# Third layer's adjacency counting in finer steps, and the sum rounds' one-hots by eight operations per batch

## The reference

```
# third: relational sum, 8 relations
xW  = einsum('ni,rio->nro', x, W)                       # W mixed from basis_w
agg = segment_sum(xW[src, etype], dst)
h   = relu(agg + x @ loop_w + bias) + relu(x @ res_w + res_b)     # then a batch norm
# fourth: two plain mean aggregations
mean = segment_sum(x[src], dst) / max(deg, 1)
y    = mean @ W_l.T + b + x @ W_r.T                     # relu after the first
```

## Time and profile before

| | |
|---|---|
| median of 3 runs | 6375.03 us (6363.15 to 6378.08) |
| the profiled execution | 6382.97 us, of which the span of instructions is 6381.1 us |
| PE, PEld, DVE, ACT, POOL busy | 4386.8, 3624.8, 2671.0, 1784.3, 4172.8 us |
| gathers of POOL | 4160, 3.9 ms of busy time |

### The profile page before, as it was taken

The page is one execution under the profiler, slowest core; times in us unless marked ns, Lnnn a source line. Parts: engine busy times, 40 slices in busy tenths (PEclk is TensorE's granted clock), DMA queues, the critical chain, the costliest instruction groups (busy, mean ns, idle before and its releaser), DMA issues. The chain is left out here.

```text
span 6381.1 us, 116473 instructions
## 1 busy us (share of the span) xinstructions
PE 4386.8 (69%) x25432; PEld 3624.8 (57%) x25433; DVE 2671.0 (42%) x9398; ACT 1784.3 (28%) x5020; POOL 4172.8 (65%) x4271
## 2 busy tenths in 40 slices
PE   4488888878877785666666765565555557776776
PEld 3377777767776774555555554444444445555554
DVE  6643333333333332666666553433344352223222
ACT  0022222222222223444444353333333330001001
POOL 3067777757777773777777656555555537776777
PEclk6599999999999996555666677777777779898988
DMA  3066666642222212333333322222222224444443
GB/s 78 3 171 158 154 158 157 156 113 53 53 53 53 53 52 47 87 84 83 83 85 83 81 60 75 72 68 63 72 73 73 71 95 139 139 132 131 132 139 101
DMA packets 383128, 595.38 MB, mean 93 GB/s; under 512 B 120483, under 2 KB 289988, under 8 KB 372420
## 3 DMA queue, kind: packets, MB, share of 16 engines
q0 software_dynamic: 133120, 276.30, 16.9%
q1 hardware_dynamic: 245156, 310.79, 16.5%
q10 hardware_dynamic: 4128, 1.75, 0.1%
HBM read 519.07 MB, written 69.42 MB: 92 GB/s over the span
## 5 line engine op out<-in xcount | busy, mean ns | idle before, releaser
L1404 PE MATMUL PS<-ROOM 128*128 128x128 f32 x8320 | 1058.4, 287 | 171.9 <-ACT ROOM L1010 103.5
L1404 PEld LDWEIGHTS PS<-ROOM 128*128 128x128 f32 x8320 | 999.2, 199 | 237.4 <-ACT ROOM L1010 124.1
L839 POOL DMA_INDIRECT GB<-table,IDX x832 | 801.1, 963 | 393.6 <-issue 245.9
L1010 ACT COPY ROOM<-PS 128x512 f32<-128x512 f32 x1040 | 609.9, 586 | 890.5 <-PE PS L1418 890.1
L839 POOL DMA_INDIRECT ROOM<-table,IDX x416 | 402.7, 968 | 376.4 <-ACT IDX L986 252.2
L839 POOL DMA_INDIRECT GB<-in_x,IDX x416 | 402.9, 969 | 370.8 <-ACT IDX L986 234.7
L2058 DVE TENSOR_TENSOR ROOM<-ROOM,PS 128x128 f32 x312 | 89.6, 287 | 1121.4 <-PE PS L1429 1107.2
L811 POOL DMA_INDIRECT GB<-table,IDX x416 | 417.0, 1002 | 170.9 <-issue 125.2
L1346 PE MATMUL PS<-PACK 128*128 128x300 bf16 x624 | 186.8, 396 | 479.3 <-ACT SPARE L981 253.7
L799 POOL DMA_INDIRECT GB<-table_gat,IDX x416 | 429.1, 1032 | 127.7 <-issue 124.7
L811 POOL DMA_INDIRECT ROOM<-table,IDX x416 | 418.1, 1005 | 126.8 <-issue 125.9
(11 more groups left out here) (410 smaller groups left out, 8165.0 us busy)
## 6 DMA issues: line engine op xcount, KB each, us to landing
H<-one_over SPq DMA_DIRECT2D x416, 128.0 KB
ROOM<-one_over SPq DMA_DIRECT2D x416, 128.0 KB
neighbours<-ROOM SPq DMA_DIRECT2D x26, 1700.0 KB, 6.3
ROOM<-neighbours SPq DMA_DIRECT2D x26, 1700.0 KB
PACK<-neighbours SPq DMA_DIRECT2D x26, 1700.0 KB
ROOM<-local_row SPq DMA_DIRECT2D x104, 256.0 KB
GB<-table,IDX POOLq DMA_INDIRECT x1248, 2.5
ROOM<-table,IDX POOLq DMA_INDIRECT x832
```

What stands on the lines that cost most here:

```text
L839: pool.indirect_dma_start(out=r.rows[c][:, j * P:(j + 1) * P], out_offset=None, in_=r.dram[:, :], in_offset=bass.IndirectOffsetOnAxis(ap=I ...
L1010: act.copy(to.rearrange("p r (j d) -> p r j d", j=r.per), of.rearrange("p (j d r) -> p r j d", j=r.per, d=NEAR))\
L1404: ins = nc.tensor.matmul(PS[:, 4, 0:P], r.near[1 - b][:, t * P:(t + 1) * P], r.weights[:, t * P:(t + 1) * P], start=t == 0, stop=t == r.re ...
```

## The change

1. `meta_of` no longer has its loaded values checked against their bounds at run time (all rounds, all engines that call it).
2. Counting in round c: PE does tile 0 ahead of L1404, tile 1 in its middle, tile 2 behind it, tiles 3 and 4 behind the two units, tile 5 behind L1429. ACT takes out 0 and 1 ahead of its copy L997, and 2 behind it. A take-out waits only for the correction that frees its side column. DVE loads offsets and makes the low part ahead of L2058, and then alternates one correction and one key of the next step, four pairs ahead of L2058 and the rest behind it. The low part has a second buffer.
3. The mixed rounds' one-hots are made by eight `tensor_scalar` of 128 columns where one `tensor_tensor` of 8 x 128 was.
4. SP stores the rows ahead of the first two loads of matrices in mixed round a (in round b the order stays).

```diff
@@ meta_of
-                                                                 engines=[engine.engine], min_val=0, max_val=most)
+                                                                 engines=[engine.engine], min_val=0, max_val=most,
+                                                                 skip_runtime_bounds_check_because="VectorE clamps what meta holds")
@@ load_all
+                if m.n == 0:
+                    store_rows(t, f)
                 for e in range(2):
                     load(m, e, e)
-                store_rows(t, f)
+                if m.n == 1:
+                    store_rows(t, f)
@@ ACT take_out, near_round      (FREE_OF = [-5] * 5 + [-4] * 5 + [-4] * 6)
-                if n == 0 and (not isinstance(t, int) or t > 0):
-                    act.wait_ge(mx_cor, t)
+                if not isinstance(t, int) or FREE_OF[j] + t > 0:
+                    act.wait_ge(mx_cor, d * PAIR + (j + FREE_OF[j]))
...
+                    tiles = TILES_OF[c] if counting and now < BATCHES else range(0)
+                    if tiles:
+                        offsets = offsets_of(act, i, tiles)
+                        for n in range(2):
+                            take_out(i, n, tiles[n], offsets)
                     if 1 <= now <= BATCHES:
...
                         act.copy(MADE[1 - b][:, :], PS[:, 4, 0:P]).then_inc(made_sb, 1)
-                    tiles = TILES_OF[c] if counting and now < BATCHES else range(0)
                     if tiles:
-                        offsets = offsets_of(act, i, tiles)
-                        for n in range(2):
-                            take_out(i, n, tiles[n], offsets)
+                        take_out(i, 2, tiles[2], offsets)
...
-                                for at in range(2 + 2 * n, 4 if n == 0 else len(tiles)):
+                                for at in range(3 + n, 4 if n == 0 else len(tiles)):
@@ PE near_round
+                    if tiles:
+                        count_tile(i, c, 0, tiles[0])
...
+                            if tiles and 2 * t + 2 == r.rels:
+                                count_tile(i, c, 1, tiles[1])
                         ins.then_inc(made_ps, 1)
...
-                        for n in range(2):
-                            count_tile(i, n, tiles[n])
+                        count_tile(i, c, 2, tiles[2])
...
-                                for at in range(2 + 2 * n, 4 if n == 0 else len(tiles)):
-                                    count_tile(i, at, tiles[at])
+                                count_tile(i, c, 3 + n, tiles[3 + n])
...
+                    for n in range(5, len(tiles)):
+                        count_tile(i, c, n, tiles[n])
@@ DVE near_round
+            def key_tile(d, c, n):
+                column = bass.ds(d * (CYCLE * G) + TILES_OF[c][n], 1)
+                dve.tensor_scalar(HOT_KEY[n], iota_h[:, :], near_col[:, column], None, ALU.is_equal).then_inc(mx_hot, 1)
+            def correct(d, c, n, offset):
+                j = TILES_OF[c][n]
+                dve.wait_ge(mx_out, d * PAIR + (j + 1))
...
+                    if counting and now < BATCHES:
+                        offsets = offsets_of(dve, i, TILES_OF[c]) if TILES_OF[c] else []
+                        if TILES_OF[(c + 1) % FOUR]:
+                            low_tiles(i, (c + 1) % FOUR)
+                        count_some(i, c, range(0, 4), offsets)
                     if 1 <= now <= BATCHES:
...
                     if counting and now < BATCHES:
-                        mine, later = TILES_OF[c], TILES_OF[(c + 1) % FOUR]
-                        if mine:
-                            offsets = offsets_of(dve, i, mine)
-                            dve.wait_ge(mx_out, i * PAIR + (mine[-1] + 1))
...
+                        count_some(i, c, range(4, HOTS), offsets)
+                def count_some(i, c, some, offsets):
+                    mine, later = TILES_OF[c], TILES_OF[(c + 1) % FOUR]
+                    for n in some:
+                        if n < len(mine):
+                            correct(i, c, n, offsets[n])
+                        if n < len(later):
+                            key_tile(i, (c + 1) % FOUR, n)
@@ hot_sparse
-                    dve.tensor_tensor(OH[:, b, :].rearrange("p (j n) -> p j n", j=G), mid(iota_f[:, :], G),
-                                      last(local[:, bass.ds(n, G)], P), ALU.is_equal).then_inc(mx_oh, 1)
+                    for j in range(G):
+                        ins = dve.tensor_scalar(oh(b, j), iota_f[:, :], local[:, bass.ds(n + j, 1)], None, ALU.is_equal)
+                    ins.then_inc(mx_oh, 1)
```

More of the change, by code:

```diff
@@ L317, in build @@
                     SPARE[:, (b - 4) * KEYS // 2:(b - 3) * KEYS // 2]).bitcast(BF16) for b in range(HOTS)]
-        HOT_LO = PACK[:, ROWB * P + 2 * KEYS:ROWB * P + 2 * KEYS + HOTS * P // 2].bitcast(BF16).rearrange("p (j n) -> p j n", j=HOTS)
         SIDE = SPARE[:, KEYS:KEYS + HOTS * NHI // 2].bitcast(BF16).rearrange("p (j h) -> p j h", j=HOTS)
+        low_at = KEYS + HOTS * NHI // 2
+        HOT_LO = [at.bitcast(BF16).rearrange("p (j n) -> p j n", j=HOTS)
+                  for at in (PACK[:, ROWB * P + 2 * KEYS:ROWB * P + 2 * KEYS + HOTS * P // 2], SPARE[:, low_at:low_at + HOTS * P // 2])]
         MADE_UP = ROOM[:, 2 * NODES_P + R8 * P:2 * NODES_P + R8 * P + COUNTED].bitcast(BF16)
@@ L1398, in step @@
                             wide(k, b)
+                    tiles = TILES_OF[c] if counting and now < BATCHES else range(0)
+                    if tiles:
+                        count_tile(i, c, 0, tiles[0])
+                        if isinstance(k, int) and k == 0:
+                            count_tile(i, c, 1, tiles[1])
                     if 1 <= now <= BATCHES:
@@ L1935, in _, with low_tiles @@
             dve.reciprocal(inv_degree[:, :], inv_degree[:, :]).then_inc(degree, 1)
-            def hot_tiles(d, tiles, some):
-                n0 = d * (CYCLE * G) + tiles[0]
+            def low_tiles(d, c):
+                tiles = TILES_OF[c]
                 m = len(tiles)
-                if some[0] == 0:
-                    dve.tensor_tensor(HOT_LO[:, 0:m, :], mid(iota_h[:, 0:P], m), last(lo_col[:, bass.ds(n0, m)], P), ALU.is_equal)
-                for n in some:
-                    dve.tensor_scalar(HOT_KEY[n], iota_h[:, :], near_col[:, bass.ds(n0 + n, 1)], None, ALU.is_equal).then_inc(mx_hot, 1)
-            def correct(d, tiles, offsets):
-                for n, j in enumerate(tiles):
-                    if j == 0:
-                        dve.sem_inc(mx_cor, 1)
-                        continue
-                    dve.wait_ge(mx_cor, d * PAIR + j)
-                    column = MADE_HALVES[:, :, :, bass.ds(offsets[n], 1)].rearrange("p a h o -> p (a h) o")
-                    dve.tensor_tensor(column, column, SIDE[:, n, :].unsqueeze(2), ALU.add).then_inc(mx_cor, 1)
+                dve.tensor_tensor(HOT_LO[c % 2][:, 0:m, :], mid(iota_h[:, 0:P], m),
+                                  last(lo_col[:, bass.ds(d * (CYCLE * G) + tiles[0], m)], P), ALU.is_equal)
+            def key_tile(d, c, n):
[4 more added lines that the diff above has]
+                dve.wait_ge(mx_out, d * PAIR + (j + 1))
+                if j == 0:
+                    dve.sem_inc(mx_cor, 1)
+                    return
+                dve.sem_inc(near_passed, 1)
+                dve.wait_ge(mx_cor, d * PAIR + j)
+                column = MADE_HALVES[:, :, :, bass.ds(offset, 1)].rearrange("p a h o -> p (a h) o")
+                dve.tensor_tensor(column, column, SIDE[:, n, :].unsqueeze(2), ALU.add).then_inc(mx_cor, 1)
             def near_round(r, mix=None, counting=False):
@@ L2062, in step @@
                     if counting and now < BATCHES:
-                        mine, later = TILES_OF[c], TILES_OF[(c + 1) % FOUR]
-                        if mine:
-                            offsets = offsets_of(dve, i, mine)
-                            dve.wait_ge(mx_out, i * PAIR + (mine[-1] + 1))
-                            dve.sem_inc(near_passed, 1)
-                        if later:
-                            hot_tiles(i, later, range(2))
-                        if mine:
-                            correct(i, mine, offsets)
-                        if later:
-                            hot_tiles(i, later, range(2, len(later)))
+                        count_some(i, c, range(4, HOTS), offsets)
[6 more added lines that the diff above has]
+                            key_tile(i, (c + 1) % FOUR, n)
                 hot(0, 0, 1)
```

7 lines of the change are left out of this document (4 added, 3 removed).

## The result

The changed kernel takes 5916.36 us (median of 4 runs, 5913.5 to 5917.11); the kernel before took 6376.56 us on the same chip (4 runs, 6363.15 to 6391.31). The ratio is 0.9277, 95% interval 0.9256 to 0.9298: 460 us less. The forecast was 5955, with a range from 5920 to 6060.

What follows compares the result with a forecast made beforehand. Round c was taken as bound by a chain through the engines, other gather stages by POOL's issue. From 6382.97 us, less 46, 2, 337 and 41, came 5957; less 8 for the profiled execution, 5949, rounded to 5955; range 5920 to 6060.

Steps and rivals of the forecast that it cites:

- Bound and mechanism: Round c: a chain through the engines sets the 54.46 us cycle; once shortened, POOL takes over by a small margin.
- Part 2: Round c: reordered counting steps cut the cycle from 54.46 to 41.5 us, 26 times, a gain of 337 us.
- The rival "POOL never waits": Round c: 1061 us of gathers plus about 20 behind, 350 us gained, total 5935; chance 0.17.
- 41.5: Round c: forecast us per cycle, above POOL's 40.8 because PE waits for rows in mid-step; bounds 40.3 and 46.
- 6 us of rounding at the sum: Total: 5949 raised to 5955, since a chain and a resource within 3 us rarely meet without loss.
- 38.3: Round c: forecast us per cycle for the new chain of four steps, 2.5 us under POOL's 40.8.
- ACT's load ahead of take-out 0: Round c, steps 2 and 3: ACT's offset load, covered by nothing, priced at 1.9 us from the dearest case.
- Part 1: Removed checks: 46 us less in the counting of degrees and 2 us in SP's first windows.
- 0.56 us less of sequencer time takes away 0.32 and 0.56 of these: 0.88 for two batches: Counting of degrees: removed checks shorten the "issue" waits of DVE's add L1882, 52 times, 46 us.
- Part 3: Mixed rounds: eight short one-hot operations leave 8 of 49 us of gather excess, a gain of 41 us.
- the case that was feared: Mixed rounds: the eight operations hinder POOL more, a 17 us loss, 58 us above forecast, total 6013; chance 0.07.
- Part 4: SP's stores ahead of loads in mixed round a: gain 0, with 11 us of cover for the loads.

Runs made afterwards that it cites:

- half the gathers: Round c issues 4 of 8 gathers per batch: on the kernel after 5717.43 us, after with checks back 5887.62, kernel before 6361.52.
- part 2 alone: Kernel before with only the finer counting steps of round c, checks, single one-hot operation and SP's old order kept: 6022.95 us, ratio 0.9444.
- part 1 alone: Kernel before with only the run-time checks in meta_of removed, on all engines: 6193.84 us, ratio 0.9711.

## Why the prediction went as it did

**Bound and mechanism: right.** Round c was a chain through the engines (half the gathers: 54.6 in place of 54.8 us a cycle), the new order shortened it below POOL's pace, and POOL took over.

**Part 2, -350.8 for -337: nearly right, and in part by luck.** The time after was met: 26 x 41.5 is 1079 us, and from the first gather of round c to its last sum (L2058, now L2083) it takes 1082. What was short is the time before: 26 cycles like the one shown, of 54.46 us, are 1416 us, and the round took 1431.9, with a mean cycle of 54.8 behind its first three. The rival took 1431.6 and gave 350. That 41.5 was met is luck in its last part: it was POOL's 40.8 and 0.7 for the meeting with the chain, and no such loss came. POOL's own cycle is 41.2, because its gathers are 0.984 us long and not 0.970; with the low parts made by short operations it is 40.4. So the 6 us of rounding at the sum ("a chain and a resource that are within 3 us of each other rarely meet without loss") had no ground either. The chain is 33.5 us with half the gathers, and not 38.3; the distance to POOL is 7.7 us and not 2.5. By its own pieces: steps 1 and 2 were put at 8.0 + 1.9 = 9.9 us each and took 8.8 and 8.4; steps 3 and 0 were put at 18.5 and took 16.6. The take-outs themselves were nearly right: in step 1, 6.86 us from first to last start and 0.83 for the last, with the index copy behind it, make 7.7, put at 8.0. What was too dear was ACT's load ahead of take-out 0: 1.9 us, from the dearest load there was the earlier trace rows, while the gap on the timeline above is 1.16 us. A dearest case is an end of a range, not the price of each step. Also, the pieces were timed at a clock of 0.75 and ran at 0.95 in that run, so part of the difference may be the clock's.

**Part 1, -72 for -48: here the prediction failed most. The mechanism was right, the term was mis-sized.** The step that failed is "0.56 us less of sequencer time takes away 0.32 and 0.56 of these: 0.88 for two batches": it lets only the add's own wait shrink, and never below nothing. DVE's timeline in the counting of degrees, a pair of batches, after (rows 7 have before):

```profile
199.88 0.27 DVE L1897 TENSOR_TENSOR ROOM<-ROOM,PS 16x128 f32 x1
200.13 0.29 DVE L1928 TENSOR_TENSOR ROOM<-iota_w,etype 128x128 bf16<-128x128 f32 x1
200.34 1.22 DVE L1929 TENSOR_TENSOR OH<-iota_w,local 128x1024 bf16<-128x1024 f32 x1
201.59 0.28 DVE L1897 TENSOR_TENSOR ROOM<-ROOM,PS 16x128 f32 x1
...
203.35 0.27 DVE L1897 TENSOR_TENSOR ROOM<-ROOM,PS 16x128 f32 x1
```

A pair now takes 203.35 - 199.88 = 3.47 us, and took 4.79: 1.32 us and not 0.88, 52 times, 69 us. (POOL's 33rd gather comes 3 us earlier still, in what lies between the counting and it.) The add's idle time fell from 56.8 to 5.8 us over the stretch, 51 us, which is the 46 of the forecast. Two more things were in the rows and not in the sum. The operation behind the add (L1913 before, with waits of 0.21 and 0.15 us) stood idle for 18.6 us in all, of which 11 went. And in every second batch the add now starts before the 1.22 us operation has ended (at 199.88; 198.75 + 1.22 is 199.97), 0.09 us 52 times, another 5 us: idle time that falls to nothing need not stop at zero. What became of the checks, in the source view of L589 over the whole run:

```profile
L589 DVEq TENSOR_LOAD <-meta x1145: 300/317/1530, 42.9 to 5875.3; - x191
L589 DVEq FUSED_REGOPS  x923: 53/65/129, 48.4 to 5819.2; - x185
```

The asserts are gone, and the register work is a third in number (2798 before) and in length (median 190 ns before): the check's own work does go with it, as taken. That nothing is gained elsewhere held for near round b, and for the mixed rounds with their new one-hots (1042.3 us with the checks, 1042.5 without). For attention it did not: a stage in which POOL issues without pause still has gathers that DVE holds up, and without the checks DVE's operations fall beside more of them: 13.6 us lost, 10 in the mean of all runs, for which the forecast had no term.

**Part 3, -45.5 for -41: right.** The gathers of the changed kernel, mixed rounds:

```profile
L818 POOL DMA_INDIRECT GB<-table,IDX x416: 940/944/1267, 4794.5 to 5847.6; - x139
```

The longest is 1.27 us where it was 1.96; 4 us of excess remain, not 8. What the prediction made of the rule in the Trainium skill ("SBUF — State Buffer", section "SBUF: two separate sides") was incomplete: it read the two-source operation as the harmless kind, and went by its own rows against that, rightly. That page sets an operation with two SBUF inputs against a GpSimd operation that reads SBUF, and the gathers here do read their indices there (`GB<-table,IDX`). It also says that the shared ports are held for the whole instruction, and with that the runs with one long operation agree: a gather that starts beside it waits for all of it but the last 0.12 us. That a one-source fp32 operation may hold POOL up as well, the runs bear out for a long one, and more widely than the two-source one does (22 of 22 gathers under way against 0 of 30); but eight short ones, the case that was feared, cost 0.02 us a batch.

**Part 4, 0: right.** From the last gather of round c to the first of mixed round a it is 54.0 us with SP's old order (part 2 alone) and 54.0 with the new one. The gap between the mixed rounds, where the order is the same, is 27.9 to 31.6 us in the kernels with the old order and 28.1 to 31.5 in those with the new, so the 3.7 us are scatter.

**The range.** From 5955 to 5916 it is 39 us: 24 in the counting of degrees, 14 in round c, 6 of rounding, 4.5 in part 3 and 12 in smaller stretches, less 14 of attention and less 8 by which the profiled execution of before stood above its median (that of after did not). Without the 24 us the time would lie inside the range. The term was priced from the add's wait alone; the prediction's own 0.28 us a value, for four values and nothing hidden, makes 1.12 us a pair and 58 us. The rival "POOL never waits" had its margin from a chain whose pieces were all taken dear, so 0.17 was too little for it, and the low end of 5920 left no room for two terms being better at once.

## What to carry to other kernels

When a chain is taken apart and a resource becomes the bound, price the resource by its own rows and each piece of the chain by its usual duration, and keep dearest cases for the range; with the 7.7 us of margin there was here, the meeting of the two cost nothing. Take the time before from the whole stretch, and not from one cycle of it times their number. When sequencer work goes from a serial loop, start from all of it and ask what could hide it, rather than from one operation's wait. Two edits that shorten the same chain don't add up once the resource bounds it (part 1 is worth 189 us alone and some 60 behind part 2), so ask of each edit what it is worth behind the other. And in stages that a descriptor-making GpSimd bounds, cut long VectorE operations beside it into short ones, one-source operations where there is a choice: the total may even grow. Then look at the single gathers again, for short two-source operations in a row can still hold one up to the last of them.

## What the runs showed of the hardware

- A gather's issue on POOL is 0.945 us alone. One that starts beside a single long VectorE operation is held until 0.12 to 0.13 us before that ends, be it a `tensor_tensor` of 1.22 us (87 of 87) or a `tensor_scalar` of 0.75 us (69 of 74). One already 0.1 to 0.48 us under way is held by the `tensor_scalar` only (22 of 22, against 0 of 30). In sum: 0.45 us a batch for one of 1.22 us, 0.14 for one of 0.81, 0.08 for eight `tensor_tensor` of 0.28 us each that start 0.2 us apart, 0.02 for eight such `tensor_scalar`.
- Short two-source operations in a row can hold a gather to the last of them: 29 of 111 gathers beside attention's eight, up to 1.2 us, and two beside the mixed rounds' eight, up to 1.78 us. Short one-source operations did so in none of 139.
- A run-time check of one loaded value cost VectorE's sequencer 0.28 us by the asserts of rows 5 and 0.33 by the counting of degrees (1.32 us for four values); all engines' checks together cost 4.0 us a cycle of round c's chain in the new order (37.5 to 33.5 us), 3.9 in the old one (54.8 to 50.9 us).
- The granted clock of round c, with the same matmuls: 0.73 at 54.8 us a cycle, 0.86 at 41.2, 0.95 at 33.5. It does not go by the length of a cycle alone: with part 1 alone it is 0.69 at 50.9 us.
